# Linear stage's PReLU: one ScalarE eviction and two VectorE operations per block, in place of two ScalarE passes and one VectorE operation

## Chip, cores and metric

The kernel runs on one core of a Trainium2 chip. A core has a matrix engine (TensorE, in the profile PE for matmuls and PEld for weight loads), VectorE (DVE), ScalarE (ACT), GpSimd (POOL) and a queue engine SyncE (SP) that issues the DMAs here. Each engine runs its own list of instructions in order; a wait stands in front of an instruction and holds back all that is queued behind it on that engine. SBUF is the on-chip memory, PSUM holds the matmul results in banks. The metric is the device time of one execution in microseconds (us); lower is better.

## What is computed

A block of a graph network with 1250 nodes of 512 features: a layer norm, then a GNN branch, an attention branch and a gated feed-forward. What the change touches is the first step of the GNN branch, the linear layer with a PReLU whose slope differs by feature:

```python
def _prelu(x, a):
    return jnp.where(x > 0, x, a * x)
...
x = _prelu(x @ lin_W.T + lin_b, lin_a)          # [1250, 512], lin_a has one slope per output feature
for l in range(L):
    agg = jax.ops.segment_sum(x[src], dst, num_segments=n)
    h = x + agg
    h = _prelu(h @ conv_W1[l].T + conv_b1[l], conv_a[l])
    ...
xn = _layernorm(x, axis=-1)
x = x + _L0_gnn_ref(xn, ...) + _L0_mix_ref(xn[None], ...)[0]
x = x + _L0_ffn_ref(_layernorm(x, axis=-1)[None], ...)[0]
```

## The kernel before

**Number format.** Matrices are multiplied as two float16 parts, a rounded one ("high") and the rest ("low"), with three matmuls per product (`passes`, L459 is its matmul line). So most tiles are evicted twice: ScalarE writes the high part, VectorE or GpSimd subtracts it from the full value to make the low part.

**The linear stage.** The 1250 nodes go in J = 5 chunks of CH = 250 (a chunk is a pair of 125-row tiles); the 512 output features go in KB = 4 blocks of 128. For a chunk j and a block m TensorE runs 12 matmuls of 128x250 into PSUM bank m (`product`, L459). After block 2 of a chunk it transposes the two normalised tiles of the next chunk (`flip_pair`, L524). Those transposes wait for the normalised tiles (`xn_nat`), which ScalarE makes for the first two pairs (L805) and GpSimd for the last three (L1718, `POOL_NORM = 2`). The transposed tiles are evicted by ScalarE (L811, high part) and VectorE (L1167, low part), and the next chunk's matmuls wait for the latter.

**Per block of the linear output**, ScalarE reads the PSUM bank twice: `lin_neg = relu(-(y + b))` (L828) and `lin_t = relu(y + b)` (L829); the second frees the bank. VectorE then makes `lin_t = lin_neg * (-a) + lin_t` (L1236, `lin_chunk`), counted by the semaphore `lin_out`. ScalarE rounds the result to float16 (`high_in`, L837, waits for `lin_out`), GpSimd subtracts (L1737, the low part). `lin_neg` has one slot per block, so L828 of chunk j waits for `lin_out` of chunk j - 1.

**Order on ScalarE, chunk j**: blocks 0 and 1 of chunk j; `high_in` of blocks 2 and 3 of chunk j - 1; a standard deviation (L795); the two transposed tiles of the next chunk (L811); blocks 2 and 3; `high_in` of blocks 0 and 1. In chunk 1 the weight rounding of the next stage follows (L777, 128x2048), in chunk 3 a table load (L868). **Order on VectorE**: the low parts of a pair (L1167), row statistics of a later pair (L1189), the four L1236 of a chunk, the reciprocal that GpSimd's normalising waits for (L1214), and, spread between the last chunks, four quarters of the low part of the next stage's weights (`low_up0`, L1168); the fourth raises `w_split`, for which the next stage's first matmul waits, and so does SP's DMA of the weights after (L401).

**The stage behind** (`up_tile`, L459 with 128x512 matmuls, ten tiles of 12 matmuls, two PSUM banks in turn): a bank is free when VectorE's low part (`low_up`, L1168, output 125x512) is done. Between the end of the linear stage and the first of those, VectorE prepares the edge lists (L1281 to L1285).

The same PReLU stands in the two GNN layers in the other form: one ScalarE eviction (L948), then on VectorE `min(t, 0) * a` (L1440) and `max(t, 0) + that` (L1444), `prelu_pair`; GpSimd makes the low part there too (L1754).

Of the kernel before, what the change touches and what calls it, by code (L numbers as in the profile page):

```python
# [23 lines left out]
ALU = mybir.AluOpType  # L24
ACT = mybir.ActivationFunctionType
# [8 lines left out]
KB = D // 128  # L34
# [28 lines left out]
S_X, S_W, S_H, S_K, S_Q, S_M = 16.0, 256.0, 1 / 16, 256.0, 1024.0, 256.0  # L63
# [43 lines left out]
def before(family, phase, who=None, high=False):  # L107

    total = 0
    for name, uses, by, hi in USES[family]:  # L110
        if name == phase:
            return total
        if (who is None or by == who) and (hi or not high):
            total += uses
    raise KeyError(phase)
# [15 lines left out]
def entry(family, phase):  # L131
    return next(u for u in USES[family] if u[0] == phase)
# [19 lines left out]
def gps_block(nc, dram):  # L152

    with ExitStack() as ctx:
        def sb(name, shape, dt=F32):
            return ctx.enter_context(nc.sbuf_tensor(name, shape, dt))

        def sem(name):
            return ctx.enter_context(nc.semaphore(name))
# [3 lines left out]
        def bank(family, slot):  # L163

            if family == "t":
                return ps[:, slot, 0:CH]
            return ps[:, {"z": 0, "n": 0, "x": 4, "y": 6}[family] + slot, :]
# [16 lines left out]
        def tr32(r):  # L185
            return r[:, 0:KB * N].rearrange("p (k n) -> p k n", k=KB)

        def tr16(r, blocks=KB):
            return r[:, 0:blocks * N].bitcast(F16).rearrange("p (h k n) -> p h k n", h=2, k=blocks)

        xn_nat, xn_t = nat32(r5), tr16(r1)
        lin_t, in_t = tr32(r3), tr16(r4)
# [58 lines left out]
        stat = sb("stat", [128, KB * J * 6])  # L251
        mv = sb("mv", [128, T, 2])
        std = sb("std", [128, T])
        lin_minus = sb("lin_minus", [128, 2 * KB])
        eps = sb("eps", [128, 3])
        rstd = sb("rstd", [128, T])
        shift = sb("shift", [128, T])
# [9 lines left out]
        bias_a, lin_bias = sb("bias_a", [128, 2 * KB]), sb("lin_bias", [128, KB])  # L267
# [17 lines left out]
        lin_neg = prep[:, 3000:3000 + KB * CH].rearrange("p (m n) -> p m n", m=KB)  # L285
        first_i = prep[0:NWIN, 2802:2803].bitcast(I32)

        def col(name, i=0, n=1):
            return cols[:, COL[name][0] + i:COL[name][0] + i + n]
# [9 lines left out]
        def sems(*names):  # L299
            return (sem(n) for n in names)  # L300

        w_scaled, w_high, w_split = sems("w_scaled", "w_high", "w_split")
        lin_high, lin_low, lin_neg_ready = sems("lin_high", "lin_low", "lin_neg_ready")
        consts, iotas = sems("consts", "iotas")
        dve_step, pool_step = sems("dve_step", "pool_step")

# [13 lines left out]
        lin_out, prelu_out, hid_high, tmp_free, bias_ready, layer_out, first_out = sems(  # L321
            "lin_out", "prelu_out", "hid_high", "tmp_free", "bias_ready", "layer_out", "first_out")
# [9 lines left out]
        def wait_full(eng, family, phase, i):  # L332
            eng.wait_ge(full[family], before(family, phase) + i + 1)
# [4 lines left out]
        def wait_done(eng, family, phase, n):  # L338

            who = entry(family, phase)[2]  # L340
            eng.wait_ge(free[family, who], RING[family] + before(family, phase, who) + n)

        def wait_bank(pe, family, phase, i, slot):

            names = [u[0] for u in USES[family]]
            _, _, who, _ = entry(family, phase)
            pe.wait_ge(free[family, who], before(family, phase, who) + i + 1)
            if names.index(phase):
                last, uses, by, _ = USES[family][names.index(phase) - 1]  # L350
                if by != who:
                    pe.wait_ge(free[family, by], before(family, last, by) + uses + slot + 1)
            if phase in BANKS_FROM:
                source, last, uses = BANKS_FROM[phase]
                if slot < min(RING[family], RING[source]):
                    wait_done(pe, source, last, uses + slot)
# [70 lines left out]
        def _(pe):  # L427
# [8 lines left out]
            def window(phase, i):  # L436

                w = first_window(phase) + i
                slot = w % 2
                pe.wait_ge(off_ready, w + 1)  # L440
                _, at = nc.values_load_multi_w_load_instructions(
                    offsets[0:1, slot, :], engines=[mybir.EngineType.PE], min_val=0, max_val=WK - SPAN,
                    skip_runtime_bounds_check_because="clamped to the window where they are made")
                pe.wait_ge(adj_freed, w + 1)
                nc.tensor.matmul(ps[:, 6 + slot, 0:WK], zeros[:, :], iota_mem[0:1, 0:WK], start=True, stop=False)  # L445
                pe.wait_ge(oh_ready, w + 1)
                for c in range(WC):
                    mm_ = nc.tensor.matmul(ps[:, 6 + slot, bass.ds(at[c], SPAN)], oh_s[:, slot, c, :], oh_d[:, slot, c, :],  # L448
                                           start=False, stop=(c == WC - 1))
                mm_.then_inc(adj_full, 1)  # L450
# [310 lines left out]
        def _(act):  # L761
# [59 lines left out]
            def lin_blocks(j, blocks):  # L821

                chunk = slice(j * CH, (j + 1) * CH)
                for m in blocks:
                    wait_full(act, "t", "lin", KB * j + m)
                    if j:
                        act.wait_ge(lin_out, KB * (j - 1) + m + 1)
                    nc.scalar.activation(lin_neg[:, m, :], bank("t", m), ACT.Relu, bias=lin_minus[:, m:m + 1], scale=-1 / S_W)  # L828
                    nc.scalar.activation(lin_t[:, m, chunk], bank("t", m), ACT.Relu, bias=lin_bias[:, m:m + 1], scale=1 / S_W  # L829
                                         ).then_inc(free["t", "act"], 1)  # L830

            def high_in(j, blocks):
# [6 lines left out]
            def normalize_pair(g):  # L839
                act.wait_ge(norm_ready, TURN["xn"] + g + 1)  # L840
                for t in (2 * g, 2 * g + 1):
                    normalize(xn_nat, x, t)
# [7 lines left out]
                high_lin(m)  # L850
            deviations(2, 4, TURN["xn"] + 1, scaled=1)
            normalize_pair(1)
            act.wait_ge(lin_neg_ready, 1)
            for j in range(J):
                lin_blocks(j, (0, 1))
                if j:
                    high_in(j - 1, (2, 3))
                if j + 2 < HT:
                    deviations(2 * j + 4, 2 * j + 6, TURN["xn"] + j + 2, scaled=1)
                if j + 1 < HT:  # L860
                    for t in (2 * j + 2, 2 * j + 3):
                        high_tile_t("xn", xn_t, t)
                lin_blocks(j, (2, 3))
                high_in(j, (0, 1))
                if j == 1:
                    high_weight("up0", S_W)
                if j == J - 2:
                    nc.scalar.preload_act_table(ACT.Exp)  # L868
# [254 lines left out]
        def _(dve):  # L1123
# [10 lines left out]
            def first_columns(w):  # L1134

                _, at = nc.values_load_multi_w_load_instructions(
                    window_at[0:1, w:min(w + AT_ONCE, NWIN)], engines=[mybir.EngineType.DVE], min_val=0, max_val=COLS,
                    skip_runtime_bounds_check_because="a count of at most COLS heads, less one, and not below zero")
                column.extend(at)
# [65 lines left out]
            def deviation_of(g):  # L1205
                dve.wait_ge(got_x[g], 32)
                pair_statistics(x, g)
# [23 lines left out]
            def lin_chunk(j):  # L1231

                chunk = slice(j * CH, (j + 1) * CH)
                for m in range(KB):
                    wait_done(dve, "t", "lin", KB * j + m + 1)
                    nc.vector.scalar_tensor_tensor(lin_t[:, m, chunk], lin_neg[:, m, :], lin_minus[:, KB + m:KB + m + 1],  # L1236
                                                   lin_t[:, m, chunk], ALU.mult, ALU.add).then_inc(lin_out, 1)

            dve.wait_ge(iotas, 1)
            nc.vector.tensor_copy(iota_mem[:, 0:WK], iota_i[:, 0:WK])  # L1240
# [9 lines left out]
            low_lin(2)  # L1250
            low_lin(3)
            dve.wait_ge(got_cols, 16)
            nc.vector.tensor_scalar(lin_minus[:, 0:KB], col("lin_b", 0, KB), -S_X, None, ALU.mult)
            nc.vector.tensor_scalar(lin_minus[:, KB:], col("lin_a", 0, KB), -1.0, None, ALU.mult)
            nc.vector.tensor_scalar(lin_bias[:, :], col("lin_b", 0, KB), S_X, None, ALU.mult).then_inc(lin_neg_ready, 1)
            dve.wait_ge(lin_neg_ready, 1)
            deviation_of(2)
            low_pair(1)
            reciprocal_of(2)
            deviation_of(3)  # L1260
            lin_chunk(0)
            reciprocal_of(3)
            low_pair(2)
            deviation_of(4)
            lin_chunk(1)
            reciprocal_of(4)
            low_pair(3)
            low_up0(0)
            lin_chunk(2)
            low_up0(1)  # L1270
            low_pair(4)
# [594 lines left out]
```

## Time and profile before

| | before |
|---|---|
| median of 3 runs | 514.51 us (512.54 to 516.02) |
| the profiled execution | 516.56 us |
| its span in the trace | 514.8 us, mean granted clock 0.969 |
| PE busy | 473.1 us, 92% |
| PEld busy | 359.3 us, 70% |
| DVE busy | 324.3 us, 63% |
| ACT busy | 250.6 us, 49% |
| POOL busy | 166.2 us, 32% |
| chain that ended last | PE 77%, DVE 13%, ACT 5%, issue 3%, POOL 1%, DMA 1% |

TensorE sets the time: the chain of work that ended last runs through it for 77% of the span. The linear stage lies at 12 to 49 us of the span, the stage behind it at 49 to 80 us. The profiled execution took 1.8 us more than its span, and 2.05 us more than the median of the three runs.

### The profile page before, as it was taken

How to read it: one execution, taken by the hardware profiler on the slowest of the kernel's cores; microseconds unless marked ns; L12 is line 12 of the kernel's file. 1: busy time of each engine (PE TensorE's matmuls, PEld its weight loads, DVE VectorE, ACT ScalarE, POOL GpSimd, SP SyncE). 2: the span in 40 equal slices, each digit the busy share in tenths (PEclk: the TensorE clock that was granted, in tenths of full speed). 3: DMA queues.
4: the chain of work that ended last, by engine and by line, in shares of the span. 5: the costliest groups of instructions: out<-in, count | busy, mean ns of one | idle time of the engine just before them, and what ended most of it. 6: DMA issues, size and time to landing. Idle time of an engine off the chain costs nothing.

```text
span 514.8 us, 9887 instructions
## 1 busy us (share of the span) xinstructions
PE 473.1 (92%) x3564; PEld 359.3 (70%) x3564; DVE 324.3 (63%) x749; ACT 250.6 (49%) x524; POOL 166.2 (32%) x176
## 2 busy tenths in 40 slices
PE   2989999999999998997999997999999979989893
PEld 1768568877765675654999994668998758956641
DVE  4766698748999837653654447635333675439787
ACT  4787344156722354334344755424346377734454
POOL 1469243030193011033235990003232123304402
PEclk9989999999999989998999998999999969989998
DMA  8701002202020002022000001000000295000014
GB/s 244 202 3 51 32 1 83 83 1 81 2 83 1 2 1 83 0 83 73 13 0 0 1 2 60 1 0 1 0 1 5 81 406 248 1 0 2 1 48 151
DMA packets 5246, 27.44 MB, mean 53 GB/s; under 512 B 1036, under 2 KB 1161, under 8 KB 3544
## 3 DMA queue, kind: packets, MB, share of 16 engines
q1 hardware_dynamic: 5208, 26.92, 15.2%
q8 instruction: 25, 0.41, 0.3%
q14 instruction: 13, 0.11, 0.1%
HBM read 24.36 MB, written 2.56 MB: 52 GB/s over the span
## 4 chain that ended last, share of the span: by engine, by line
PE 77%; DVE 13%; ACT 5%; issue 3%; POOL 1%; DMA 1%; SPq 0%; ACTq 0%; DVEq 0%
PE ps L459 47%; PE ps L628 17%; PE ps L448 4%; PE ps L725 3%; PE ps L524 2%; PE ps L445 1%; PE ps L534 1%; DVE r L1665 1%; DVE r L1167 1%; DVE r L1677 1%; POOL late L1718 1%; DVE ohs L1158 1%; DVE r L1655 1%; DMA x<-in_x 1%; DVE offsets L1153 1%
## 5 line engine op out<-in xcount | busy, mean ns | idle before, releaser
L459 PE MATMUL ps<-r,wslot 128*128 128x250 f16 x840 | 98.1, 277 | 4.4 <-DVE r L1167 4.3
L459 PEld LDWEIGHTS ps<-r,wslot 128*128 128x128 f16 x840 | 83.0, 100 | 16.8 <-DVE r L1167 5.9
L628 PE MATMUL ps<-late,r 125*128 (+1 forms) x800 | 88.7, 272 | 3.5 <-issue 3.5
L628 PEld LDWEIGHTS ps<-late,r 125*128 125x128 f16 x800 | 78.3, 98 | 14.2 <-issue 4.2
L1726 POOL TENSOR_TENSOR wslot<-stage,wslot 128x512 f16<-128x512 f32 x32 | 39.5, 1266 | 140.6 <-ACT wslot L777 140.6
L459 PE MATMUL ps<-wslot,r 128*125 128x512 f16 x300 | 69.3, 381 | 0.0
L459 PE MATMUL ps<-wslot,late 128*125 128x512 f16 x240 | 56.4, 389 | 3.0 <-DVE late L1459 2.7
L1754 POOL TENSOR_TENSOR late<-ohs,late 128x250 f16<-128x250 f32 x40 | 25.7, 652 | 94.3 <-ACT late L953 94.3
L459 PEld LDWEIGHTS ps<-wslot,r 128*125 128x125 f16 (+1 forms) x300 | 39.3, 136 | 22.4 <-issue 2.3
L459 PE MATMUL ps<-late,wslot 128*128 (+1 forms) x480 | 51.7, 269 | 0.0
L459 PEld LDWEIGHTS ps<-late,wslot 128*128 128x128 f16 x480 | 46.6, 97 | 5.3 <-issue 0.8
L788 ACT ACTIVATE late<-ps 125x500 f16<-125x500 f32 x25 | 14.7, 587 | 69.2 <-PE ps L448 69.2
L459 PEld LDWEIGHTS ps<-wslot,late 128*125 128x125 f16 x240 | 32.6, 139 | 22.2 <-DVE late L1459 3.0
L1440 DVE TENSOR_SCALAR ohs<-ohs,cols 128x250 f32<-128x250 f32 x40 | 16.1, 406 | 47.1 <-ACT ohs L948 47.1
L948 ACT ACTIVATE ohs<-ps,bias_a 128x250 f32<-128x250 f32 x40 | 18.6, 467 | 35.5 <-PE ps L628 29.6
L1168 DVE SCALAR_TENSOR_TENSOR r<-ps,r 125x512 f16<-125x512 f32 (+1 forms) x30 | 20.3, 683 | 24.4 <-ACT r L801 16.9
L801 ACT ACTIVATE r<-ps 125x512 f16<-125x512 f32 x20 | 12.0, 599 | 35.5 <-PE ps L459 35.5
L1148 DVE TENSOR_TENSOR ohs<-iota,sources 125x1920 f16<-125x1920 f16 x25 | 28.8, 1151 | 0.1
L1000 ACT ACTIVATE r<-ps,cols 128x250 f32<-128x250 f32 x40 | 18.2, 465 | 20.0 <-PE ps L459 20.0
L459 PE MATMUL ps<-late,r 128*125 128x512 f16 x120 | 27.4, 380 | 0.0
L448 PEld LDWEIGHTS ps<-ohs 125*128 125x128 f16 x375 | 19.0, 97 | 8.1 <-issue 5.6
L448 PE MATMUL ps<-ohs 125*128 125x70 f16 x375 | 24.4, 198 | 0.0
(183 smaller groups left out, 732.3 us busy)
## 6 DMA issues: line engine op xcount, KB each, us to landing
late<-in_tv SPq DMA_DIRECT2D x2, 4096.0 KB, 18.3
x<-in_x SPq DMA_DIRECT2D x5, 448.0 KB
out<-r SPq DMA_DIRECT2D x10, 224.0 KB
stage<-in_w_up SPq DMA_DIRECT2D x2, 1024.0 KB, 5.3
stage<-in_w_down SPq DMA_DIRECT2D x2, 1024.0 KB, 5.5
stage<-in_w_lin SPq DMA_DIRECT2D x1, 1024.0 KB, 6.2
stage<-in_w_k SPq DMA_DIRECT2D x1, 1024.0 KB, 4.8
stage<-in_w_q SPq DMA_DIRECT2D x1, 1024.0 KB, 4.8
```

The lines of the kernel that those rows point to most:

```text
L448: mm_ = nc.tensor.matmul(ps[:, 6 + slot, bass.ds(at[c], SPAN)], oh_s[:, slot, c, :], oh_d[:, slot, c, :], start=False, stop=(c == WC - 1))
L459: last = nc.tensor.matmul(out, stat_(hs, b), mov(hm, b), start=start and n == 0, stop=stop and n == 3 * blocks - 1)
L628: last = nc.tensor.matmul(bank("t", m), u_nat[layer][:, p, h, m * 128:(m + 1) * 128], counts(h)[:, chunk], start=(start and h == 0 and p = ...
L725: last = nc.tensor.matmul(bank_, g_diag[:, k, :], part(E - PE_EXPERTS + k), start=(k == PE_EXPERTS - share), stop=(k == PE_EXPERTS - 1))
L788: nc.scalar.activation(adj[:, :, w * WIN:(w + 1) * WIN], ps[0:P, 6 + w % 2, 0:WK].rearrange("p (d h) -> p h d", h=T), ACT.Copy, accum_out= ...
L948: nc.scalar.activation(act_tmp[:, m, :], bank("t", m), ACT.Identity, bias=bias_a[:, KB * layer + m:KB * layer + m + 1], scale=S_H / S_X).t ...
L1000: nc.scalar.activation(gnn_t[:, m, j * CH:(j + 1) * CH], bank("t", i % KB), ACT.Identity, bias=col("b2", KB * layer + m), scale=1 / (S_W * ...
L1148: nc.vector.tensor_tensor(oh_s[:, slot].rearrange("p c (s r) -> p c s r", r=RUN), iota_s.unsqueeze(1).to_broadcast([P, WC, 128 // RUN, RUN ...
L1168: return nc.vector.scalar_tensor_tensor(out, src, scale, hi, ALU.mult, ALU.subtract)
L1440: nc.vector.tensor_scalar(negative[:, q, :], act_tmp[:, q, :], 0.0, col("conv_a", layer), ALU.min, ALU.mult).then_inc(neg_ready, 1)
L1726: last = nc.gpsimd.tensor_tensor(wslot[:, i % SLOTS, 1, k, :], stage[:, k * D:(k + 1) * D], wslot[:, i % SLOTS, 0, k, :], ALU.subtract)
L1754: nc.gpsimd.tensor_tensor(a_t[:, 1, m, chunk], act_tmp[:, m, :], a_t[:, 0, m, chunk], ALU.subtract).then_inc(tmp_free, 1)
```

## The change

Per block, the ScalarE pass L828 goes, and with it the wait for `lin_out` of the chunk before. L829 becomes an eviction without the relu (bias and scale as they were). VectorE makes the PReLU in two operations, in pairs of blocks: twice `lin_neg = min(lin_t, 0) * a`, then twice `lin_t = max(lin_t, 0) + lin_neg`. The constants `lin_minus` and the two small VectorE operations that made them go.

```diff
-                    if j:
-                        act.wait_ge(lin_out, KB * (j - 1) + m + 1)
-                    nc.scalar.activation(lin_neg[:, m, :], bank("t", m), ACT.Relu, bias=lin_minus[:, m:m + 1], scale=-1 / S_W)
-                    nc.scalar.activation(lin_t[:, m, chunk], bank("t", m), ACT.Relu, bias=lin_bias[:, m:m + 1], scale=1 / S_W
+                    nc.scalar.activation(lin_t[:, m, chunk], bank("t", m), ACT.Identity, bias=lin_bias[:, m:m + 1], scale=1 / S_W
                                          ).then_inc(free["t", "act"], 1)
...
-            act.wait_ge(lin_neg_ready, 1)
+            act.wait_ge(lin_bias_ready, 1)
...
             def lin_chunk(j):
 
                 chunk = slice(j * CH, (j + 1) * CH)
-                for m in range(KB):
-                    wait_done(dve, "t", "lin", KB * j + m + 1)
-                    nc.vector.scalar_tensor_tensor(lin_t[:, m, chunk], lin_neg[:, m, :], lin_minus[:, KB + m:KB + m + 1],
-                                                   lin_t[:, m, chunk], ALU.mult, ALU.add).then_inc(lin_out, 1)
+                for lo in (0, 2):
+                    for m in (lo, lo + 1):
+                        wait_done(dve, "t", "lin", KB * j + m + 1)
+                        if j:
+                            dve.wait_ge(lin_out, KB * (j - 1) + m + 1)
+                        nc.vector.tensor_scalar(lin_neg[:, m, :], lin_t[:, m, chunk], 0.0, col("lin_a", m), ALU.min, ALU.mult
+                                                ).then_inc(lin_min, 1)
+                    for m in (lo, lo + 1):
+                        dve.wait_ge(lin_min, KB * j + m + 1)
+                        nc.vector.scalar_tensor_tensor(lin_t[:, m, chunk], lin_t[:, m, chunk], 0.0, lin_neg[:, m, :],
+                                                       ALU.max, ALU.add).then_inc(lin_out, 1)
...
-            nc.vector.tensor_scalar(lin_minus[:, 0:KB], col("lin_b", 0, KB), -S_X, None, ALU.mult)
-            nc.vector.tensor_scalar(lin_minus[:, KB:], col("lin_a", 0, KB), -1.0, None, ALU.mult)
```

On ScalarE, from the last two blocks of chunk 1 on (`late` holds `lin_neg` and the float16 inputs of the next stage, `r` holds `lin_t` and the transposed tiles), there stood before:

```order
L828 ACTIVATE late<-ps,lin_minus 128x250
L829 ACTIVATE r<-ps,lin_bias 128x250
L837 ACTIVATE late<-r 128x250 x2
L777 ACTIVATE wslot<-stage 128x2048
L828 ACTIVATE late<-ps,lin_minus 128x250
L829 ACTIVATE r<-ps,lin_bias 128x250
L828 ACTIVATE late<-ps,lin_minus 128x250
L829 ACTIVATE r<-ps,lin_bias 128x250
L837 ACTIVATE late<-r 128x250 x2
```

and of the changed kernel, at the same place (line numbers move up by 1 to 4):

```order
L825 ACTIVATE r<-ps,lin_bias 128x250 x2
L833 ACTIVATE late<-r 128x250 x2
L776 ACTIVATE wslot<-stage 128x2048
L825 ACTIVATE r<-ps,lin_bias 128x250 x2
L833 ACTIVATE late<-r 128x250 x2
```

Two of four evictions went between the weight rounding and the next roundings; nothing else changed its place.

On VectorE, from the fourth weight quarter (L1168) over chunk 4 to the edge lists, there stood before:

```order
L1168 SCALAR_TENSOR_TENSOR wslot<-stage,wslot 128x4x128 [waits w_high]
L1236 SCALAR_TENSOR_TENSOR r<-late,lin_minus,r 128x250 [waits t_free_act] x4
L1281 TENSOR_SCALAR heads<-late 125x330 [waits got_edges]
L1282 CAST late<-late 25x1
L1283 TENSOR_SCALAR late<-heads,late 25x330 [waits dve_step]
```

and of the changed kernel:

```order
L1164 SCALAR_TENSOR_TENSOR wslot<-stage,wslot 128x4x128 [waits w_high]
L1235 TENSOR_SCALAR late<-r,cols 128x250 [waits lin_out,t_free_act] x2
L1239 SCALAR_TENSOR_TENSOR r<-r,late 128x250 [waits lin_min] x2
L1235 TENSOR_SCALAR late<-r,cols 128x250 [waits lin_out,t_free_act] x2
L1239 SCALAR_TENSOR_TENSOR r<-r,late 128x250 [waits lin_min] x2
L1282 TENSOR_SCALAR heads<-late 125x330 [waits got_edges]
```

Four instructions became eight, and the first finished block of a chunk now comes third instead of first. The other four chunks change in the same way.

## Rows read from the trace of the kernel before

**Rows 1.** Totals of waiting, 12 to 60 us: who waited <- for whom, us, times, longest
```profile
PE ps L459 <- DVE r L1167: 4.3, 4, 2.3
PE ps L524 <- POOL late L1718: 0.5, 1, 0.5
```

**Rows 2.** Timeline, 20 to 36 us: start, us, engine, line, operation, tiles, count, [idle before]
```profile
20.08 4.75 POOL L1718 TENSOR_SCALAR late<-x,mv,rstd 125x512 f32<-125x512 f32 x2 [17.35 <-DVE rstd L1214]
21.35 1.62 DVE L1236 SCALAR_TENSOR_TENSOR r<-late,lin_minus,r 128x250 f32<-128x250 f32 x4
...
25.15 4.13 POOL L1718 TENSOR_SCALAR late<-x,mv,rstd 125x512 f32<-125x512 f32 x2 [0.32 <-DVE rstd L1214]
...
28.26 1.61 DVE L1236 SCALAR_TENSOR_TENSOR r<-late,lin_minus,r 128x250 f32<-128x250 f32 x4
28.74 0.80 ACT L837 ACTIVATE late<-r 128x250 f16<-128x250 f32 x2 [1.06 <-DVE r L1236]
29.45 1.89 ACT L777 ACTIVATE wslot<-stage 128x2048 f16<-128x2048 f32 x1
...
31.25 0.45 ACT L828 ACTIVATE late<-ps,lin_minus 128x250 f32<-128x250 f32 x1
...
31.95 0.47 ACT L828 ACTIVATE late<-ps,lin_minus 128x250 f32<-128x250 f32 x1
...
33.45 1.07 ACT L811 ACTIVATE r<-ps 128x500 f16<-128x500 f32 x2
...
34.08 1.26 DVE L1167 TENSOR_TENSOR r<-ps,r 128x500 f16<-128x500 f32 x2 [0.32 <-ACT r L811]
```

**Rows 3.** A stretch of PE: from:to, length, busy (instructions), granted clock, DMA share, GB/s
```profile
35.40:39.10 3.70, 3.70 (x19) 0.54 0.02 4
```

**Rows 4.** Timeline, PE alone, 19 to 36 us
```profile
19.96 4.01 PE L459 MATMUL ps<-r,wslot 128*128 128x250 f16 x36 [0.28 <-DVE r L1167]
```

**Rows 5.** The chain that ended last, 35 to 42 us
```profile
35.40 5.68 PE ps L459 x36
```

**Rows 6.** Timeline, 39 to 55 us, the end of the linear stage
```profile
43.95 3.26 DVE L1236 SCALAR_TENSOR_TENSOR r<-late,lin_minus,r 128x250 f32<-128x250 f32 x4
...
46.09 1.28 ACT L868 ACT_TABLE_LOAD   x1
47.13 1.14 DVE L1168 SCALAR_TENSOR_TENSOR wslot<-stage,wslot 128x512 f16<-128x512 f32 x1
...
48.62 5.34 PE L459 MATMUL ps<-wslot,late 128*125 128x512 f16 x24
...
51.48 0.79 DVE L1281 TENSOR_SCALAR heads<-late 125x330 f32<-125x330 int32 x1
...
53.52 0.68 DVE L1168 SCALAR_TENSOR_TENSOR r<-ps,r 125x512 f16<-125x512 f32 x1
...
54.25 2.80 PE L459 MATMUL ps<-wslot,late 128*125 128x512 f16 x12 [0.28 <-DVE r L1168]
```

**Rows 7.** Timeline, POOL alone, 20 to 56 us
```profile
39.09 15.02 POOL L1737 TENSOR_TENSOR late<-r,late 128x250 f16<-128x250 f32 x20
```

**Rows 8.** Timeline, DVE, first GNN layer: the new form with GpSimd idle
```profile
246.28 0.35 DVE L1440 TENSOR_SCALAR ohs<-ohs,cols 128x250 f32<-128x250 f32 x1 [2.12 <-ACT ohs L948]
246.54 0.74 DVE L1444 SCALAR_TENSOR_TENSOR ohs<-ohs 128x250 f32<-128x250 f32 x2
247.20 1.28 DVE L1483 BATCH_NORM_STATS2 stat<-r 125x6 f32<-125x512 f32 x2
```

**Rows 9.** Timeline, DVE and POOL, both GNN layers: the new form with GpSimd busy
```profile
281.23 2.89 DVE L1444 SCALAR_TENSOR_TENSOR ohs<-ohs 128x250 f32<-128x250 f32 x2
...
282.51 1.33 POOL L1761 TENSOR_TENSOR x<-x,r 125x512 f32<-125x512 f32 x1
...
353.66 1.04 DVE L1440 TENSOR_SCALAR ohs<-ohs,cols 128x250 f32<-128x250 f32 x2 [0.84 <-ACT ohs L948]
```

**Rows 10.** Source view of L1737: count, durations in ns, min/median/max
```profile
L1737 POOL TENSOR_TENSOR late<-r,late x20: 657/743/1131, 39.1 to 53.4; 128x250 f16<-128x250 f32 x20
```

More of the change, by code:

```diff
@@ L253, in gps_block @@
         std = sb("std", [128, T])
-        lin_minus = sb("lin_minus", [128, 2 * KB])
         eps = sb("eps", [128, 3])
@@ L303, in gps_block @@
         w_scaled, w_high, w_split = sems("w_scaled", "w_high", "w_split")
-        lin_high, lin_low, lin_neg_ready = sems("lin_high", "lin_low", "lin_neg_ready")
+        lin_high, lin_low, lin_bias_ready, lin_min = sems("lin_high", "lin_low", "lin_bias_ready", "lin_min")
         consts, iotas = sems("consts", "iotas")
@@ L1252, in _ @@
             dve.wait_ge(got_cols, 16)
-            nc.vector.tensor_scalar(lin_minus[:, 0:KB], col("lin_b", 0, KB), -S_X, None, ALU.mult)
-            nc.vector.tensor_scalar(lin_minus[:, KB:], col("lin_a", 0, KB), -1.0, None, ALU.mult)
-            nc.vector.tensor_scalar(lin_bias[:, :], col("lin_b", 0, KB), S_X, None, ALU.mult).then_inc(lin_neg_ready, 1)
-            dve.wait_ge(lin_neg_ready, 1)
+            nc.vector.tensor_scalar(lin_bias[:, :], col("lin_b", 0, KB), S_X, None, ALU.mult).then_inc(lin_bias_ready, 1)
+            dve.wait_ge(lin_bias_ready, 1)
             deviation_of(2)
```

## Prediction

> **What bounds the kernel now.** The table of busy shares and the chain that ended last say TensorE: 92% busy, 77% of the chain. So only TensorE's idle time in the linear stage, and what it does to the next stage, can pay or cost. I read the totals of waiting for 12 to 60 us first [rows 1]: TensorE's matmuls wait 4.3 us for VectorE's low parts of the transposed tiles (L1167; the longest wait is 2.3 us), and 0.5 us for GpSimd's normalising. Nobody on TensorE waits for ScalarE's double evictions or for L1236 directly. Then the timeline around the long wait [rows 2]: the low parts at 34.08 wait for the ScalarE eviction L811 at 33.45, which is queued behind two blocks of double evictions from 31.25, behind the weight rounding L777 (29.45, 1.89 us), behind two L837 that waited 1.06 us for the first L1236 of chunk 1 at 28.26. 
> The second place is the end of the stage [rows 6]. The fourth weight quarter on VectorE (47.13, done at 48.27) is done 0.35 us before the next stage's first matmul at 48.62. The third tile of that stage starts at 54.25, 0.28 us after TensorE was free, because VectorE's first low part there comes at 53.52, behind the edge lists that begin at 51.48, right after the last L1236. VectorE has no slack at all here.
>
> **Prices.** ScalarE loses 20 instructions. From one L828 to the next, with an L829 between, it is 0.70 us (31.25, 31.95) [rows 2], so a pass costs 0.35 us: 7.0 us of ScalarE in all, 0.70 us for two blocks. VectorE: four L1236 start 0.38 to 0.39 us apart when nothing disturbs them ((1.61 - 0.47)/3, the last one's 0.47 being its own length) [rows 2], 1.56 us per chunk. The new form exists in the GNN layers: L1440 to L1444 is 0.26 us, and two L1444 take 0.66 us to the next start [rows 8]. A chunk becomes 4 x 0.27 + 4 x 0.33 = 2.40 us, 0.84 us more, 4.2 us in all. The two small operations that made the constants go too; they lie behind TensorE's first blocks, so that is worth nothing.
>
> Undisturbed is not the rule. From 39.09 to 54.1 us GpSimd runs its twenty L1737 without a pause [rows 7], and beside it the four L1236 of chunk 3 take 3.26 us, that is one per 0.80 us instead of 0.39 [rows 6], while an L1737 goes from 0.66 us to 0.74 in the median [rows 10]: the two engines take turns. The new pair is not spared: two L1444 beside 1.3 us tensor_tensors of GpSimd took 2.89 us instead of 0.74, and two L1440 1.04 instead of 0.71 [rows 9]. What a turn costs on top is 0.41 us (0.80 - 0.39), so I take 0.67 us for a disturbed L1440-form and 0.74 for a disturbed L1444-form. The more instructions, the more turns: that is what the change adds at the end of the stage. The bounds for a chunk are 2.4 us (no turn lost) and 5.6 us (all lost), against 3.2 now.
>
> **Sum, first place (chunks 0 to 2).** In a chunk the first finished block now comes third: at 28.26 + 0.27 + 0.27 + 0.41 = 29.21 and the second at 29.54, so L837 runs until 29.88 and L777 starts 0.43 us later than at 29.45. Then two evictions fall away, -0.70. L811 starts at 33.18, the low parts at 33.81, the matmuls at 35.13: **-0.27 us**. The wait is 2.05 us instead of 2.32, so I let the clock fall as before: 0 us. Ahead of that, L811 and L1167 of the pair before hang on GpSimd's L1718 that ends at 24.83 [rows 2]; it moves only if VectorE delays it. The pair at 25.15 took 4.13 us and the one at 20.08, beside the L1236 of chunk 0, 4.75 [rows 2], so L1236 may have cost it 0.6 us. I leave it as it is, with -0.6 (it gets its normal length) and +0.8 (two more turns of 0.41 us lost) as bounds.
>
> **Second place (chunks 3 and 4).** Chunk 3 starts 0.27 us earlier, at 43.68. GpSimd has blocks in stock for the next 4 us, so six of the eight operations lose a turn: 0.67 x 2 + 0.74 x 2 + 0.67 x 2 = 4.2 us, to 47.8. By then GpSimd has used up its stock. Blocks 2 and 3 of chunk 3 reach it only when ScalarE has rounded them, behind blocks 0 and 1 (to about 46.9), the table load (1.28 us [rows 6]) and two evictions (0.70): 48.9 for the start, 49.2 for the first. The last two operations and the weight quarter run undisturbed (0.66 and 0.68 us) and `w_split` comes at 49.1, not 48.3. The next stage begins at 49.1 instead of 48.6 (TensorE would be ready at 48.35). SP's next weight DMA stands behind the same semaphore and moves too, by 0.8 us; its data is wanted only in the seventh tile of the stage behind. Chunk 4 starts at 49.0; its evictions come in time, since ScalarE has shed 0.7 us per pair of blocks. GpSimd resumes at about 49.2 with four to six blocks, and I count four of eight turns as lost: 2.4 + 4 x 0.41 = 4.0 us, to 53.0. The edge lists follow (2.0 us) and the first low part comes at 54.9 instead of 53.52. The third tile starts 1.4 us later than at 54.25. The gain of the first place is already in this, as chunk 3's earlier start: **+1.4 us in all**. Behind it I see no work whose time doesn't hang on TensorE, so nothing is given back. Bounds: with no turn lost in either chunk, VectorE is done at 50.0 and TensorE runs through, -0.6 us; with all lost, `w_split` comes at 50.4 and VectorE ends chunk 4 at 56.0, +4.5 us.
>
> The profiled execution of before took 516.56 us; the sum by it is 518.0. The median is 2.05 us lower, so I forecast 515.9 us for the median, rounded 516.
>
> **Rivals.**
> *GpSimd's long tensor_scalar blocks the new one (slower).* In chunks 0 to 2 the new L1440-form meets L1718 (4.13/2 = 2.07 us each). Would each of them hold VectorE off until it ends, chunk 0 would end at about 26.6 instead of 22.9 (one operation at 22.15, the rest behind the second L1718), and the low parts behind it 1.1 us late; chunk 1 would meet the next pair, L777 would start 3.2 us late, L811 3.2 - 0.7 = 2.5 us late, and chunk 2 would wait for 2 us more, in which TensorE has work. The sum is 2.5 + 1.4 to 4.5, in the middle 5.5 us, 520 us. It decides from about 2 us of blocking in chunk 1 on. Against it: the four L1236 at 21.35, which also read two tensors from SBUF, ran through L1718 in 1.62 us, as fast as alone [rows 2].
> The Trainium skill, page "SBUF — State Buffer", section "Who interferes with whom", says that a tensor_scalar of VectorE from SBUF to SBUF may take the port pair it shares with GpSimd, that two SBUF inputs contend with GpSimd's reads, and that the second to issue fully blocks until the first is finished. By that rule this rival would be the outcome; the trace bears it out beside L1737 and not beside L1718.
> *The clock falls once more.* The stage behind now starts with TensorE idle for 0.75 us and again 1.2 us before the third tile. If the granted clock falls there as it did after the 2.3 us wait [rows 3], it costs the same 1.67 us: 516 + 1.7 = 517.6 us. Against it: both waits are shorter.
> *Faster.* If the shorter first wait (2.05 us) leaves the clock at 2.4 GHz, 1.67 us come back, 514.2; if moreover GpSimd hinders little at the end, -0.6 takes the place of +1.4, 512.2 us. For it: ScalarE is the engine relieved. Against it: 0.27 us is little.
>
> **How the numbers follow.** The forecast 0.5, its own range 514.5 to 517.5; blocked by L1718 0.12 (520); one more fall of the clock 0.18 (517.6); faster 0.2 (512 to 514.2). The range 512.5 to 520 leaves out the far ends of the bounds (+4.5 together with a fall of the clock) and half of the last rival. A measurement can tell about 1% (5 us) from no change. Faster than that needs more than the whole best case: 0.03. Slower by that needs the blocking at its full price, or all turns lost and the clock: 0.1. Within 1%: 0.87.
>
> **What would show it.** In the profile after: L1239 and L1235 at 0.33 and 0.27 us apart in chunks 0 and 1, more in chunks 3 and 4; L776 0.4 us later and the first matmul after the long wait 0.3 us earlier; the clock near 0.54 behind it; a wait of TensorE for the weight quarter or at the start of the stage behind, and more than 1 us before its third tile, which starts at about 55.6. It is wrong if chunk 0 to 2 take far more than 2.4 us, if L1718 grows, or if the third tile starts before 54.5.

## The result and the profile after

| | before | after |
|---|---|---|
| median | 513.83 us (511.90 to 516.02, 8 runs) | 517.99 us (514.36 to 520.93, 8 runs) |
| ratio | | 1.0068, 95% interval 1.0038 to 1.0098 |
| span of the profiled execution | 514.8 us | 515.8 us |
| DVE busy | 324.3 us | 332.5 us |
| ACT busy | 250.6 us | 243.5 us |
| PE busy | 473.1 us | 472.4 us |

The change costs 0.7%, 3.5 us by the ratio (2.0 to 5.0; the two medians lie 4.2 us apart). In a second set of executions the same kernel gave 1.0057 (1.0036 to 1.0079), 2.9 us. The forecast was no change beyond 1%, 516.0 us, in a range of 512.5 to 520.0; the sum behind it was +1.4 us. Both sets say about +3 us, so half of the loss was foreseen, and the rest of the text asks where the other half comes from.

In what follows, "before" and "after" are the two kernels. The totals of waiting of after, 12 to 60 us, TensorE's rows (who waited <- for whom, us in total, times, longest), to be read beside [rows 1] (L458, L1163, L523, L1719 are the L459, L1167, L524, L1718 of before):

```profile
PE ps L458 <- DVE r L1163: 4.8, 5, 2.0
PE ps L458 <- DVE wslot L1164: 1.7, 1, 1.7
PE ps L523 <- POOL late L1719: 0.4, 1, 0.4
```

A wait of 1.7 us for the fourth weight quarter is new; the longest one fell from 2.3 to 2.0 us. TensorE alone in the timeline of after:

```profile
35.77 5.68 PE L458 MATMUL ps<-r,wslot 128*128 128x250 f16 x36 [2.00 <-DVE r L1163]
...
44.05 5.29 PE L458 MATMUL ps<-r,wslot 128*128 128x250 f16 x48 [0.47 <-DVE r L1163]
51.08 7.28 PE L458 MATMUL ps<-wslot,late 128*125 128x512 f16 x32 [1.73 <-DVE wslot L1164]
```

The second stage starts at 51.08, not at 48.62 [rows 6]. Of these 2.46 us, 0.67 were there at 17 us already (its first matmul of the stage started 0.5 us later, at 12.51 instead of 11.99; this start differs between profiles of either form, 11.79 to 13.90 us over all that follow), so 1.8 us belong to the stage. VectorE in the same place:

```profile
36.22 1.07 DVE L1235 TENSOR_SCALAR late<-r,cols 128x250 f32<-128x250 f32 x2
37.21 0.73 DVE L1239 SCALAR_TENSOR_TENSOR r<-r,late 128x250 f32<-128x250 f32 x2
37.87 2.29 DVE L1235 TENSOR_SCALAR late<-r,cols 128x250 f32<-128x250 f32 x2
40.08 1.67 DVE L1239 SCALAR_TENSOR_TENSOR r<-r,late 128x250 f32<-128x250 f32 x2
...
44.51 1.41 DVE L1235 TENSOR_SCALAR late<-r,cols 128x250 f32<-128x250 f32 x2
45.84 1.67 DVE L1239 SCALAR_TENSOR_TENSOR r<-r,late 128x250 f32<-128x250 f32 x2
47.43 1.41 DVE L1235 TENSOR_SCALAR late<-r,cols 128x250 f32<-128x250 f32 x2
48.76 1.66 DVE L1239 SCALAR_TENSOR_TENSOR r<-r,late 128x250 f32<-128x250 f32 x2
50.34 0.68 DVE L1164 SCALAR_TENSOR_TENSOR wslot<-stage,wslot 128x512 f16<-128x512 f32 x1
...
54.11 0.32 DVE L1282 TENSOR_SCALAR heads<-late 125x330 f32<-125x330 int32 x1
...
55.68 0.68 DVE L1164 SCALAR_TENSOR_TENSOR r<-ps,r 125x512 f16<-125x512 f32 x1
```

Chunk 3 takes 5.83 us (44.51 to 50.34) where it took 3.18 [rows 6]: the eight operations took 0.73 us each on the average, where 0.30 is the undisturbed value: every one of them lost a turn to GpSimd. Chunk 2 takes 5.45 us (36.22 to 41.67); two of its L1235 took 2.29 us together. GpSimd beside them:

```profile
34.23 4.23 POOL L1719 TENSOR_SCALAR late<-x,mv,rstd 125x512 f32<-125x512 f32 x2 [4.02 <-DVE rstd L1210]
38.41 0.95 POOL L1733 MEMSET ctx<- 128x1024 f16 x1
39.32 10.82 POOL L1738 TENSOR_TENSOR late<-r,late 128x250 f16<-128x250 f32 x14
```

### The profile page after: what moved, and what is told of

It reads as the page before. It is cut to its first block, busy times and chain, and to the rows that moved or that the text cites. A ratio compares the mean times of both kernels' runs of the same rounds, so it can differ in the third digit from the quotient of the medians.

```text
span 515.8 us, 9885 instructions
## 1 busy us (share of the span) xinstructions
PE 472.4 (92%) x3564; PEld 357.4 (69%) x3564; DVE 332.5 (64%) x767; ACT 243.5 (47%) x504; POOL 167.1 (32%) x176
## 4 chain that ended last, share of the span: by engine, by line
PE 81%; DVE 11%; ACT 3%; issue 2%; DMA 2%; SPq 0%; DVEq 0%
PE ps L458 51%; PE ps L627 17%; PE ps L447 4%; PE ps L724 3%; DMA stage<-in_w_lin 2%; PE ps L533 2%; DVE late L1235 2%; PE ps L523 2%; PE ps L444 2%; DVE r L1163 1%; DVE r L1666 1%; DVE r L1678 1%; DVE r L1239 1%; DVE r L1656 1%; DVE wslot L1164 1%
## 5 line engine op out<-in xcount | busy, mean ns | idle before, releaser
L458 PE MATMUL ps<-r,wslot 128*128 128x250 f16 x840 | 98.0, 277 | 4.8 <-DVE r L1163 4.8
L458 PEld LDWEIGHTS ps<-r,wslot 128*128 128x128 f16 x840 | 82.8, 100 | 17.3 <-DVE r L1163 6.3
L458 PE MATMUL ps<-wslot,r 128*125 128x512 f16 x300 | 70.8, 387 | 0.0
L458 PE MATMUL ps<-wslot,late 128*125 128x512 f16 x240 | 56.4, 389 | 4.4 <-DVE late L1460 2.7
L458 PEld LDWEIGHTS ps<-wslot,r 128*125 128x125 f16 (+1 forms) x300 | 40.0, 139 | 23.1 <-issue 3.6
L458 PE MATMUL ps<-late,wslot 128*128 (+1 forms) x480 | 51.7, 269 | 0.0
L458 PEld LDWEIGHTS ps<-late,wslot 128*128 128x128 f16 x480 | 46.6, 97 | 5.3 <-issue 0.8
L458 PEld LDWEIGHTS ps<-wslot,late 128*125 128x125 f16 x240 | 32.5, 139 | 23.9 <-DVE late L1460 3.0
L800 ACT ACTIVATE r<-ps 125x512 f16<-125x512 f32 x20 | 11.9, 596 | 35.2 <-PE ps L458 35.2
L458 PE MATMUL ps<-late,r 128*125 128x512 f16 x120 | 27.4, 380 | 0.0
```

Of the source, the lines that this page charges most:

```text
L458: last = nc.tensor.matmul(out, stat_(hs, b), mov(hm, b), start=start and n == 0, stop=stop and n == 3 * blocks - 1)
```

## Experiments

Four theories. A: VectorE is late at the end of the stage, because it takes turns with GpSimd, and TensorE waits for it. B: the loss is in chunks 0 to 2. C: the granted clock later in the kernel falls more often after any shift. D: there is a cost behind the second stage that the first profile did not show. Ratios are against executions of the kernel before taken beside each set of experiments; their medians were 514.61, 514.69 and 514.40 us in the three sets. Every interval below is 1.1 to 2.4 us wide on either side, so two kernels 1 us apart are hardly told apart by their times alone; the traces carry the finer readings.

**Which chunks.** The form is chosen by the chunk, on both engines (the diff shows ScalarE's side of the first kernel; the second has `j >= 3`); the constants of the old form are kept.

```diff
+                    if j < 3:
                         nc.scalar.activation(lin_t[:, m, chunk], bank("t", m), ACT.Identity, bias=lin_bias[:, m:m + 1], scale=1 / S_W
                                              ).then_inc(free["t", "act"], 1)
+                    else:
+                        nc.scalar.activation(lin_neg[:, m, :], bank("t", m), ACT.Relu, bias=lin_minus[:, m:m + 1], scale=-1 / S_W)
+                        nc.scalar.activation(lin_t[:, m, chunk], bank("t", m), ACT.Relu, bias=lin_bias[:, m:m + 1], scale=1 / S_W
+                                             ).then_inc(free["t", "act"], 1)
```

> New form (one eviction, two VectorE operations) in chunks 0 to 2 only; chunks 3 and 4 keep two ScalarE passes and one VectorE operation. Theory A (the loss sits at the end of the stage, where VectorE and GpSimd take turns while VectorE has no slack): 0 to -0.3 us against before; in the trace the second stage's first matmul starts within 0.2 us of TensorE being free, and its third tile within 0.5 us. Theory B (the loss is in chunks 0 to 2, from GpSimd's normalising and memset holding VectorE off): +3 us or more, and w_split still late. Theory C (the loss is a matter of the granted clock later on, hit or missed by any shift): no relation to the part, +1 to +3 us here too.

Measured: 1.0020 (0.9990 to 1.0051), median 515.80 us. In its profile TensorE is 0.2 us earlier at 60 us than before.

> New form in chunks 3 and 4 only, old form in chunks 0 to 2. Theory A: the whole loss of the change, +1.5 to +3.5 us against before; the second stage's first matmul waits 1 to 2 us for w_split and the third tile starts about 2 us later than in before. Theory B: within 1 us of before. Theory C: +1 to +3 us as in the other one.

Measured: 1.0039 (1.0014 to 1.0064), median 516.43 us. TensorE's waits in its profile (L1171, L1172 are the low parts; the 3.5 us are its first, for the first weights):

```profile
PE ps L459 <- DVE r L1171: 6.4, 4, 3.5
PE ps L459 <- DVE wslot L1172: 1.3, 1, 1.3
```

The late chunks alone bring back the wait for the weight quarter, and 2.0 us (0.7 to 3.3): theory A. The early chunks show nothing in the one profile and +1.0 us in the times, with zero inside the interval; B gets at most a part of the loss. C is not excluded by this pair: it asked for +1 to +3 us in both kernels, and they gave +1.0 and +2.0. What speaks for A is the wait in the trace of the late form, which the early form does not have.

**Without the extra operation.** `lin_t = max(a * lin_t, lin_t)` is the PReLU for slopes up to 1.

```diff
-                        nc.vector.tensor_scalar(lin_neg[:, m, :], lin_t[:, m, chunk], 0.0, col("lin_a", m), ALU.min, ALU.mult)
-                        nc.vector.scalar_tensor_tensor(lin_t[:, m, chunk], lin_t[:, m, chunk], 0.0, lin_neg[:, m, :], ALU.max, ALU.add)
+                    nc.vector.scalar_tensor_tensor(lin_t[:, m, chunk], lin_t[:, m, chunk], col("lin_a", m), lin_t[:, m, chunk],
+                                                   ALU.mult, ALU.max).then_inc(lin_out, 1)
```

> One ScalarE eviction and one VectorE operation per block, max(a * t, t), which is the PReLU only while the slope is at most 1, as all of this input's are. It takes the extra VectorE operations away and leaves ScalarE relieved. If the extra VectorE time is the whole cost (theory A): faster than before by the ScalarE chain alone, 0.5 to 1 us in the stage (the 2.3 us wait before chunk 3 shrinks by 0.7 us or more, to about 1.6), and up to 1.7 us more if the clock then stays at 2.4 GHz: -0.5 to -2.5 us. Theory C: again +1 to +3 us.

Measured: 0.9956 (0.9930 to 0.9982), median 511.94 us. The long wait in its profile was 1.6 us instead of 2.3, and the clock stayed up behind it (36 matmuls in 4.01 us). So ScalarE's relief is worth 0.7 us of waiting, as expected, and the change spends it on VectorE. C asked for a loss here too; as a cost of any shift it is out.

**A late VectorE in the kernel before.**

```diff
+            for m in range(4):
+                nc.vector.tensor_scalar(lin_neg[:, m, :], lin_neg[:, m, :], 0.0, 1.0, ALU.min, ALU.mult)
             dve.wait_ge(got_edges, 64)
```

> The kernel before, with four VectorE operations of 128x250 (the form of the new min and multiply, on a tile that nobody reads any more) in front of the edge lists. It makes VectorE late by 1.1 us (undisturbed) to 2.7 us (each one losing a turn to GpSimd) and changes nothing else. Theory A: the third tile of the second stage is late by just that and the whole kernel by the same, +1.1 to +2.7 us. If lateness there is given back later: less than half of it. If it is amplified later on (other waits, the clock): more than 3.5 us.

Measured: 1.0072 (1.0047 to 1.0097), median 518.72 us, 3.7 us with an interval of 2.4 to 5.0. Its TensorE rows:

```profile
36.97 4.01 PE L459 MATMUL ps<-r,wslot 128*128 128x250 f16 x36 [2.32 <-DVE r L1167]
...
43.40 5.29 PE L459 MATMUL ps<-r,wslot 128*128 128x250 f16 x48 [0.28 <-DVE r L1167]
48.66 5.39 PE L459 MATMUL ps<-wslot,late 128*125 128x512 f16 x24
56.95 1.29 PE L459 MATMUL ps<-wslot,late 128*125 128x512 f16 x5 [2.90 <-DVE r L1168]
```

The wait at the third tile grew from 0.28 to 2.90 us, by the four operations: 2.6 us, inside the expected 1.1 to 2.7. Nothing of it was given back, as A says. The measured 3.7 us is above the 3.5 that the expectation named as the sign of an amplified delay, but its interval holds 2.6 too. So here, in the old form, the times are again about 1 us above the trace, as they are for the change. The first row matters for what follows: in this execution the clock did not fall behind the same 2.32 us wait (4.01 us for 36 matmuls instead of 5.68), and TensorE, in the old form, kept what it gained: it waited 0.28 us for chunk 4.

**The changed kernel again.**

> The changed kernel itself once more, beside the others of this call. In its profile TensorE was 1.5 us later at 60 us than before (2.16, of which 0.65 came from a later landing of the first weights), but 8 executions gave +3.5 us. The mean granted clock of the executions was 0.972 against 0.975, and 0.0033 of mean clock is one stretch of 3.4 us at 1.2 GHz, 1.7 us. Theory A plus clock: +2.5 to +4 us against before, of which 1.5 to 2 stay when the difference of the mean clock is taken off at 1.7 us per 0.0033. Theory D (a cost behind the second stage that I have not found): more than 2.5 us stay.

Measured: 1.0057 (1.0036 to 1.0079), median 517.16 us, 2.9 us. In its profile TensorE is 1.7 us late at 60 us, with the same waits (2.0, 1.7 us); the clock had fallen behind the long one here too. From 60 to 160 us TensorE is busy throughout (99.99 to 100.00 us in this profile and in those of before and after), so lateness at 60 us is neither taken up nor added to there:

```profile
60.00:160.00 100.00, 100.00 (x734) 1.00 0.13 43
```

The mean granted clock of the ten executions was 0.9736, that of the 33 of the kernel before taken beside them 0.9755. At the expectation's price (1.7 us for 0.0033) that is 1.0 us, and 1.9 stay: inside the 1.5 to 2 of "A plus clock", below the 2.5 of D. The clock's part is uncertain, since the two means differ by only 1.4 times their standard error in this set. So D has no support, and the 1.5 to 1.7 us of the stage is about half of the measured difference.

**GpSimd out of the way.** Its low part covers 2 of 250 columns; the rest is set to zero once.

```diff
+            nc.gpsimd.memset(in_t[:, 1, :, :], 0.0)
...
+                    chunk = slice(j * CH, j * CH + 2)
                     nc.gpsimd.tensor_tensor(in_t[:, 1, m, chunk], lin_t[:, m, chunk], in_t[:, 0, m, chunk], ALU.subtract
```

> The changed kernel with GpSimd's low part of the linear output cut to 2 of 250 columns per block (the others are set to zero at the start by a GpSimd memset), so that GpSimd hardly uses SBUF while VectorE runs the new form. The low part of the linear output is left out of the result by that. If taking turns with GpSimd is what makes the new form expensive: each chunk 2.4 to 2.6 us of VectorE also at the end of the stage, w_split before TensorE is free, third tile within 0.5 us of TensorE being free, and 1.5 to 2.5 us faster than the changed kernel as it is. If the count of VectorE operations alone were the cause: still 1 us or more late.

> The same cut in the kernel before, as the counterpart: the four VectorE operations of chunk 3 take 1.6 us instead of 3.26. VectorE had 0.3 us too little slack before the third tile, so 0 to -0.6 us against before. The difference of this one and the one before it is the price of the new form without GpSimd: theory A says within 0.5 us of zero.

Measured: 1.0034 (1.0009 to 1.0058) and 1.0035 (1.0011 to 1.0059), medians 515.68 and 516.45 us. Both start TensorE 1.8 us late, for a reason of its own (last section), so the pair is compared with itself: once GpSimd is out of the way the new form costs nothing that the times can tell (the means differ by -0.6 us, with 1.1 us either way). In the same set the kernel as changed is 1.5 us slower than e6, though it does not have the 1.8 us at the start; so about 3 us hang on GpSimd's work beside VectorE, the whole loss and not only the half seen in the stage. VectorE and TensorE of e6:

```profile
45.46 0.60 DVE L1235 TENSOR_SCALAR late<-r,cols 128x250 f32<-128x250 f32 x2
45.98 0.74 DVE L1239 SCALAR_TENSOR_TENSOR r<-r,late 128x250 f32<-128x250 f32 x2
46.64 0.60 DVE L1235 TENSOR_SCALAR late<-r,cols 128x250 f32<-128x250 f32 x2
47.16 0.74 DVE L1239 SCALAR_TENSOR_TENSOR r<-r,late 128x250 f32<-128x250 f32 x2
47.82 0.68 DVE L1164 SCALAR_TENSOR_TENSOR wslot<-stage,wslot 128x512 f16<-128x512 f32 x1
```

```profile
45.00 5.29 PE L458 MATMUL ps<-r,wslot 128*128 128x250 f16 x48 [0.28 <-DVE r L1163]
50.13 7.93 PE L458 MATMUL ps<-wslot,late 128*125 128x512 f16 x36
```

Chunk 3 takes 2.36 us (45.46 to 47.82), the 2.40 of the sum, and TensorE goes into the second stage and through its third tile without a wait. The turns are the cause, not the number of operations by itself.

**The weight quarter earlier.**

```diff
             low_up0(2)
+            low_up0(3).then_inc(w_split, 1)
             lin_chunk(3)
-            low_up0(3).then_inc(w_split, 1)
```

> The changed kernel with the fourth weight quarter on VectorE ahead of chunk 3's PReLU instead of behind it. The second stage's first matmul no longer waits for w_split (1.7 us in the changed kernel); VectorE has the same work, so its first low part of the second stage, and with it the third tile, comes when it did. If two waits stand in series behind one late engine: the wait moves from the first tile to the third and grows there to about 2 us, and the time stays that of the changed kernel within 0.5 us. If w_split is the cost by itself: 1.5 us faster than the changed kernel.

Measured: 1.0090 (1.0060 to 1.0119), median 519.01 us, not faster than the changed kernel and rather slower; the expectation was within 0.5 us of it. Its TensorE rows:

```profile
35.94 4.01 PE L458 MATMUL ps<-r,wslot 128*128 128x250 f16 x36 [2.00 <-DVE r L1163]
...
44.22 6.96 PE L458 MATMUL ps<-r,wslot 128*128 128x250 f16 x48 [2.13 <-DVE r L1163]
51.01 5.34 PE L458 MATMUL ps<-wslot,late 128*125 128x512 f16 x24
57.62 0.65 PE L458 MATMUL ps<-wslot,late 128*125 128x512 f16 x2 [1.26 <-DVE r L1164]
```

The wait for the quarter is gone and one of 1.26 us stands before the third tile: two waits in series behind one late engine, as expected. That VectorE would be done when it was does not hold: its first low part of the second stage comes at 56.88 instead of 55.68, because chunk 4 took 4.10 us instead of 3.16, more turns lost. The first two rows show something else as well. Here the clock did not fall behind the 2.00 us wait: 36 matmuls in 4.01 us. In the changed kernel's profile they took 5.68, and the wait for chunk 4's low part was 0.47. 5.68 - 4.01 = 1.67, and 0.47 + 1.67 = 2.14: the wait is 2.13 us. TensorE's gain is lost whole, because VectorE is not there: it comes to chunk 4's low part (42.74 in after) only from chunk 2 and a weight quarter, which ended at 42.8. What stands ahead of that low part is the same program in e9 and in after. In the old form (e4) a clock that stayed up was kept as a gain. It is the early chunks that make VectorE late here, so this may be the 1.0 us of e1, whose profile also has the 0.47 us wait before chunk 4 instead of 0.28.

**The first low part of the second stage earlier too**, ahead of the edge lists.

```diff
+            low_up(0, 0)
             dve.wait_ge(got_edges, 64)
...
-            low_up(0, 0)
```

> The same, and VectorE's first low part of the second stage ahead of the edge lists instead of behind their first five operations (2 us). Both waits of TensorE then have their work early: third tile within 0.7 us of TensorE being free, and the loss of the changed kernel against before gone: 1.5 to 2 us faster than the changed kernel, 0 to +1.5 us against before. If more is lost somewhere else: it stays 2 us or more slower than before.

Measured: 1.0105 (1.0059 to 1.0151), median 520.30 us. The expected gain did not come; it was the expectation's other branch, 2 us or more slower than before. The timeline of e10:

```profile
53.44 1.20 DVE L1239 SCALAR_TENSOR_TENSOR r<-r,late 128x250 f32<-128x250 f32 x2
54.35 0.74 ACT L833 ACTIVATE late<-r 128x250 f16<-128x250 f32 x2 [1.71 <-DVE r L1239]
...
54.99 1.06 ACT L800 ACTIVATE r<-ps 125x512 f16<-125x512 f32 x2
55.60 0.69 DVE L1164 SCALAR_TENSOR_TENSOR r<-ps,r 125x512 f16<-125x512 f32 x1 [0.96 <-ACT r L800]
...
56.35 0.88 PE L458 MATMUL ps<-wslot,late 128*125 128x512 f16 x2 [2.32 <-DVE r L1164]
```

The low part needs ScalarE's high part (L800), and that stands behind the roundings of chunk 4 (L833), which wait for VectorE's last PReLU. The edge lists had stood in time that VectorE had to wait anyway. The wait of TensorE is now 2.32 us in one piece, and the clock fell behind it.

**A better place for ScalarE's weight rounding.** It stood on the chain to the long wait [rows 2].

```diff
-                if j == 1:
-                    high_weight("up0", S_W)
...
                         high_tile_t("xn", xn_t, t)
+                if j == 2:
+                    high_weight("up0", S_W)
                 lin_blocks(j, (2, 3))
```

> The kernel before with ScalarE's rounding of the next stage's weights (128x2048, 1.9 us) moved from the end of chunk 1 to chunk 2, behind the eviction of the two transposed tiles. It stood on the chain to TensorE's 2.3 us wait. Expected: that wait falls to about 0.5 us (the low parts start 1.8 us earlier), the clock no longer falls there, VectorE waits about 1 us for the rounded weights instead, with nobody waiting for it. -1.8 us against before, up to -3.5 where the clock fell before. If the weights are then late for w_split: less than 1 us.

Measured: 0.9972 (0.9947 to 0.9998), median 513.52 us. TensorE's waits before chunks 3 and 4:

```profile
35.79 4.01 PE L459 MATMUL ps<-r,wslot 128*128 128x250 f16 x36 [0.51 <-DVE r L1167]
...
42.71 5.29 PE L459 MATMUL ps<-r,wslot 128*128 128x250 f16 x48 [0.77 <-DVE r L1167]
```

1.81 us less before chunk 3, 0.5 more before chunk 4. The clock stayed up as well (4.01 us), so this trace has a gain of 2.9 us at the third tile; the times show 1.4 us (0.1 to 2.7). Then with the two moves on VectorE as well, in the one-operation form and in the form of before:

> One eviction and one VectorE operation max(a * t, t) (right for slopes up to 1 only), with the weight rounding moved as in the moved one, and both VectorE moves. One operation alone gave -2.2 us, the move alone -1.5. Their in-stage gains overlap (the wait of 2.3 us can go only once), so -2.5 to -4 us against before.

Measured: 0.9958 (0.9931 to 0.9985), median 512.03 us, -2.2 us, just short of the expected -2.5 to -4.

> The kernel before (two ScalarE passes, one VectorE operation) with the weight rounding moved, and both VectorE moves. -1.5 to -2.5 us against before: the move's gain plus the 0.3 us at the third tile. The table of ScalarE may bound it: its evictions come late behind the table load in chunk 3. If it is no better than the move alone, VectorE was not late in the old form.

Measured: 0.9952 (0.9917 to 0.9986), median 511.25 us, -2.5 us: the old form with the moved rounding and the two moves on VectorE, right for every slope, is ahead of both kernels. It does not differ from e11: once the rounding is off the chain, the pass that the change took from ScalarE is worth nothing that can be measured. Whether the moves on VectorE add anything to e8, the intervals don't tell.

## Why the prediction came out as it did

- **First place.** The wait was to shrink by 0.27 us; it went from 2.32 to 2.00. Right, and in both profiles of the changed kernel the clock fell as assumed: 5.68 us for the 36 matmuls, as before.
- **Prices.** Undisturbed 2.40 us per chunk was forecast, 2.36 measured (e6). For a disturbed pair I took 0.67 and 0.74 us; chunk 3 shows 1.33 us for two L1235 and 1.59 for two L1239, 0.66 and 0.80. Right but for 0.06 on the second.
- **How many turns are lost.** I counted six of eight in chunk 3 and four in chunk 4. It was all eight in chunk 3 (5.83 us, not 4.8) and, with 3.16 us, about two in chunk 4. The reason for the first is chunk 2: it took 5.45 us instead of 2.4, its last block reached GpSimd only at 42.2 us, and GpSimd, itself slowed, had work in stock through all of chunk 3 (the fourteen L1738 without a pause). TensorE's wait for `w_split` was 1.73 us instead of 0.75, and the one before the third tile, forecast at more than 1 us, is too small to show (below 0.3 us; the 36 matmuls there took 8.14 us, and 7.93 in e6). VectorE's low part, and with it the third tile, came 2.16 - 0.65 = 1.5 us late, forecast 1.4. That it fits so well is luck: more turns lost in chunk 3, fewer in chunk 4, and edge lists of 1.57 us (54.11 to 55.68) instead of 2.04. GpSimd was not idle beside the edge lists; there it was GpSimd that lost, with one L1738 of 1.74 us, begun at 53.21, beside a median of 0.72:

```profile
L1738 POOL TENSOR_TENSOR late<-r,late x20: 649/724/1740, 39.3 to 56.2; 128x250 f16<-128x250 f32 x20
```

- **The sum.** +1.4 us was right for what the stage costs in an execution in which the clock falls, as in the two profiles compared (1.5 us). It was too small for the median: the intervals of both sets begin at 1.9 us, and 518.0 us lies outside the forecast's own range (514.5 to 517.5), beside the 517.6 of the rival in which the clock falls once more. The term that was too small is the clock's, set at 0 us because both kernels have the fall behind the long wait. Two things stand in its place, and neither is settled.
  - *A gain that the new form cannot keep.* Where the clock stays up behind the long wait, the old form keeps 1.67 us (e4), and the new one waits for VectorE and keeps nothing (e9). In such an execution the change costs about 1.5 + 1.7 = 3.2 us. But of the ten profiles with a wait of 2.0 to 2.3 us at this place, eight show the fall (before, after, e1, e2, e5, e6, e7, e10) and two do not (e4, e9). At that share it adds 0.3 us on the average (an estimate, 0.2 x 1.67, from few profiles). Nor does it touch e4, which is in the old form and also 1 us above its trace.
  - *More low clock in the whole execution.* The mean granted clock over the 18 executions of the changed kernel is 0.9731, over the 95 of the kernel before that were taken beside the experiments 0.9758; the difference is 0.0027, its standard error 0.0010. Among those 95, executions with 0.0033 less mean clock are 1.0 us longer. So this is about 0.8 us (an estimate), 1.4 at the 1.7 us for 0.0033 that e5's expectation used. It fits that the slowest variants have the lowest means (e9 0.9716, e10 0.9685) and that e6, the new form without the turns, has 0.9762.

  Together with the stage these give 2.6 to 3.2 us, where 2.9 and 3.5 were measured; in part the two may be one thing, since in e9 the clock that stayed up behind the first wait fell behind the next. Where in the kernel the clock falls more often, and why, no run shows.
- **Rival "GpSimd's long tensor_scalar blocks the new one".** It did not: chunk 1 ran in 2.4 us, its first four operations beside L1719, and in chunk 0 two L1235 pairs took 0.96 and 0.95 us instead of 0.60, 0.7 us in all. By the rule of the Trainium skill (page "SBUF — State Buffer", section "Who interferes with whom") an L1235 that takes the port pair second is held until GpSimd's instruction has finished. The traces do not agree beside L1719, whose instructions last 2.07 us; they agree beside a memset (last section), and beside L1738 they show the turns.
- **Rival "the clock falls once more".** In the two profiles of the changed kernel it did not fall at the second stage; in e9 it fell behind the 2.13 us wait before chunk 4 (6.96 us for 48 matmuls instead of 5.29), in e10 behind the 2.32 us before the third tile. Its price came out nearest: 517.6 us, measured 518.0 and 517.2. The place that it named is not borne out, the lower mean clock over all executions is (above). Its cause is open.
- **Rival "faster".** Its condition occurs, its gain does not: the clock can stay up behind 2.00 us (e9), and then it is worth nothing, because VectorE is the next one late.

## What to carry to other kernels

Work moved to VectorE while GpSimd works on SBUF without a pause is priced by turns, not by its length: count the instructions; here each of 128x250 lost about 0.4 us beside GpSimd's tensor_tensor (0.80 us instead of 0.39, 0.66 instead of 0.26). When executions differ by a fall of the clock, ask for each form which engine is late next if the clock stays up; a gain that one form keeps can be worth nothing in the other. A profile is one execution: compare the mean clocks of all executions before a difference of 1 us is put down to what one profile shows. And before an engine's work is cut, look whether one long instruction on its chain can simply stand elsewhere: here that alone gave 0.3% (0.5% with two moves on VectorE), and the cut alone cost 0.6 to 0.7%.

## What the runs showed of the hardware

**A VectorE cast or tensor_scalar from SBUF to SBUF ended only after GpSimd's memset beside it.** In after one L1235 took 1.63 us instead of 0.35:

```profile
37.87 1.63 DVE L1235 TENSOR_SCALAR late<-r,cols 128x250 f32<-128x250 f32 x1
```

It ended at 39.50, and GpSimd's memset, at 38.41 for 0.95 us, at 39.36 (rows in the first section). This is not a clean case, since the end of a GpSimd tensor_scalar lies beside its first 0.6 us. The kernels e6 and e7 made the clean case, without intent. VectorE's cast at the start took 0.42 us before; beside the new memset (e6, first VectorE, then GpSimd):

```profile
2.76 4.45 DVE L1243 CAST iota<-late 125x500 f16<-125x500 int32 x1 [2.76 <-POOL late L1713]
```

```profile
2.68 4.25 POOL L1731 MEMSET late<- 128x5000 f16 x1
```

The cast ended at 7.21, the memset at 6.93. TensorE's first matmul of the linear stage comes at 13.8 us in both instead of 12.0: that is the 1.8 us by which they start late. GpSimd's tensor_scalar of 2.07 us, in contrast, let a pair of VectorE's instructions through with 0.5 us lost at most (1.07 instead of 0.60, at 36.22 in after). A version of the changed kernel with the 0.95 us memset placed elsewhere was not tried; it should make chunk 2 about 1.3 us shorter (an estimate, 1.63 - 0.35).
